# Four products of the unit matrix at the top of each step of attention, up to the ninth batch

## What is computed

```python
x = x + 0.5 * ffn(layernorm(x), gate_w, expert_bias, w1, w2, w3)
x = x + attn(layernorm(x), Wq, Wk, Wv, Wo)
x = x + 0.5 * ffn(layernorm(x), gate_w, expert_bias, w1, w2, w3)

# attn: 16 heads of 8 features, no mask
q, k, v = (x @ W.T, split in heads)
out = softmax(q @ k.T / sqrt(8)) @ v ; return out @ Wo.T
```

## Time and profile before

| | us |
|---|---|
| median of three runs | 1030.36 (1030.28 to 1030.74) |
| the profiled execution | 1034.95 |
| its span, first to last instruction | 1033.1 |
| TensorE products busy | 694.8 |
| VectorE busy | 525.0 |
| ScalarE busy | 356.0 |
| GpSimd busy | 308.2 |
| mean granted clock of TensorE | 0.833 |

### The profile page before, as it was taken

The page is one execution under the profiler, slowest core; times in us unless marked ns, Lnnn a source line. Parts: engine busy times, 40 slices in busy tenths (PEclk is TensorE's granted clock), DMA queues, the critical chain, the costliest instruction groups (busy, mean ns, idle before and its releaser), DMA issues. The chain is left out here.

```text
span 1033.1 us, 14916 instructions
## 1 busy us (share of the span) xinstructions
PE 694.8 (67%) x5124; PEld 501.0 (48%) x5124; DVE 525.0 (51%) x1350; ACT 356.0 (34%) x780; POOL 308.2 (30%) x309
## 2 busy tenths in 40 slices
PE   1335787991589427878989877657687797169900
PEld 1324676981579303434444443323476796158800
DVE  5664277330144327887878889922438632024301
ACT  0001231430134203756777565327232242024300
POOL 4235322437520660001000100340232344651065
PEclk9998787995789655988999897769898899579955
DMA  4133453862466442423333342112165485256432
GB/s 116 31 111 91 112 149 90 221 187 68 127 170 182 110 127 72 143 74 109 109 107 111 93 133 88 38 34 88 38 154 141 118 225 170 49 155 188 139 97 71
DMA packets 104987, 119.74 MB, mean 116 GB/s; under 512 B 11152, under 2 KB 87440, under 8 KB 104912
## 3 DMA queue, kind: packets, MB, share of 16 engines
q1 hardware_dynamic: 87376, 95.95, 32.2%
q0 software_dynamic: 9088, 18.63, 7.7%
q10 hardware_dynamic: 8448, 4.20, 1.4%
HBM read 87.28 MB, written 31.20 MB: 115 GB/s over the span
## 5 line engine op out<-in xcount | busy, mean ns | idle before, releaser
L544 POOL DMA_INDIRECT xe<-normed_rows,idx x156 | 153.2, 982 | 292.1 <-DVE idx L430 147.2
L901 DVE TENSOR_REDUCE mx<-banks 128x2 f32<-128x512 f32 x256 | 164.4, 686 | 41.2 <-remote 15.9
L837 ACT ACTIVATE PT<-banks 128x512 f32<-128x512 f32 x256 | 141.1, 601 | 104.9 <-PE banks L809 92.3
L700 DVE TENSOR_TENSOR hidT<-banks,act 96x256 f32<-96x256 f32 (+1 forms) x92 | 34.9, 379 | 245.5 <-ACT act L671 191.7
L556 POOL DMA_INDIRECT rows<-slots_out,slot x128 | 122.8, 959 | 115.5 <-DMA slots_out<-ye 77.0
L638 PE MATMUL banks<-WR,hidT 128*128 128x128 f32 x936 | 125.6, 283 | 26.0 <-ACT ye L679 23.1
L616 PE MATMUL banks<-xeT,WR 128*128 128x256 f32 (+1 forms) x368 | 97.1, 392 | 52.8 <-issue 52.3
L638 PEld LDWEIGHTS banks<-WR,hidT 128*128 128x128 f32 x936 | 117.3, 199 | 30.2 <-issue 28.2
L796 PE MATMUL banks<-KS,QS 56*128 56x256 bf16 x256 | 75.5, 307 | 69.0 <-DVE mx L901 57.3
L516 POOL TENSOR_TENSOR rough<-var,half_power 128x16 f32<-128x16 f32 x6 | 17.6, 2928 | 309.3 <-DVE var L252 309.3
L616 PEld LDWEIGHTS banks<-xeT,WR 128*128 128x128 f32 x368 | 65.8, 214 | 60.0 <-issue 55.6
(11 more groups left out here) (153 smaller groups left out, 972.1 us busy)
## 6 DMA issues: line engine op xcount, KB each, us to landing
WR<-in_experts SPq DMA_DIRECT2D x92, 544.0 KB
stacks<-split SPq DMA_DIRECT2D x32, 384.0 KB
slots_out<-ye SPq DMA_DIRECT2D x64, 128.0 KB
QS<-stacks SPq DMA_DIRECT2D x64, 112.0 KB
KS<-stacks SPq DMA_DIRECT2D x64, 112.0 KB
normed_rows<-xn ACTq DMA_DIRECT2D x16, 256.0 KB, 2.3
xe<-normed_rows,idx POOLq DMA_INDIRECT x156
rows<-slots_out,slot POOLq DMA_INDIRECT x128
```

Of the source, the lines that this page charges most:

```text
L544: eng.indirect_dma_start(xe[:, i % XR, a, :], None, normed_rows[h], bass.IndirectOffsetOnAxis(ap=idx[h][:, tile:tile + 1], axis=0))\
L837: eng.activation(PT[:, u % 4, 1 - k].rearrange("p t n -> p (t n)"), PS[f % 3], ACT.Exp, scale=scale).then_inc(s_exp2, 1)
L901: eng.tensor_reduce(mx[:, :, e, pair], PS[3 + e][:, :].rearrange("p (q n) -> p q n", q=2), AX.X, ALU.max).then_inc(s_max, 1)
```

## The change

At the top of each step, ahead of its scores, TensorE multiplies the unit matrix with itself four times, while n is below 9. With n from -3 to 8 and eight steps that is 12 x 8 x 4 = 384 products of 128 x 128 x 128 in bf16, each with its own weight load. They write the first 128 columns of bank 7; nobody reads them, they carry no semaphore of their own, and in those rounds nothing else uses the bank. No other instruction is added, taken away or reordered. In the lines behind it the numbers rise by 3 (L796 is L799 in the changed kernel).

```diff
@@ -718,6 +718,9 @@
                 for u in range(PAIRS):
                     if now and u == 0:
                         eng.wait_ge(s_mrow[n % 3], 32 * (n // 3 + 1))
+                    if n < NB + 1:
+                        for _ in range(4):
+                            eng.matmul(PS[7][:, 0:P], identb[:], identb[:], start=True, stop=True)
                     for k in range(2):
                         largest = largest_scores(eng, maxima_of(n, u), k)
                         scores = head_scores(eng, n, u, k) if now else iter(())
```

## The result

The changed kernel took 1039.93 us, the median of 8 runs, against 1031.40 for the kernel before beside it: a ratio of 1.0068, 95% interval 1.0042 to 1.0094. Forecast were 5.8 us less; measured were about 7 us more, outside the range. A second measurement gave 1.0057 (1.0026 to 1.0087), so the sign is not in doubt.

What follows compares the result with a forecast made beforehand. No engine was full; TensorE's clock fell in most attention rounds, and VectorE bound round 2. Sum 5.2 - 0.45 + 0.7 + 0.3 = 5.75 us gained, 1030.36 to 1024.6 us; range 1019.5 to 1031.5.

Steps and rivals of the forecast that it cites:

- The clock: TensorE in rounds 1 and 3 to 8: the added products keep full clock; 5.2 us gained in six rounds; chance 0.70.
- Rival C: Rounds 1 to 8, u = 2 to 4: products don't count for the clock, falls stay; about 5 us lost, 1035.3; chance 0.14.
- D: Clock falls move to half of the rounds instead of going away; 1.8 us gained, 1028.6; chance 0.10.
- The products' own time: Each step's four products on TensorE: 0.06 us each, 0.25 us for four at full clock.
- their place: Products on the path at u = 1 and 7, 0.2 us each, and u = 5, 0.05; elsewhere hidden; 0.45 us a round.
- the row of 24: Products in a row at the start, at half clock: about 2.4 us, delaying the second batch's L739 to some 353.5.
- The rounds 1 to 8: Attention rounds: 5.2 us gained in six rounds, 0.45 lost in round 7, 0.7 gained in round 2.
- The six rounds that had falls: Rounds 1, 3, 4, 5, 6 and 8: from 1.31 above round 7's time to 0.45 above; 5.2 us gained.
- round 7: The round already at full clock throughout, 15.90 us: it loses 0.45 us to the products.
- round 2: Round bound by VectorE: products hidden, clock may still fall once or twice; 0.3 to 1.2 us gained, 0.7 taken.
- The rounds -1 and 0: Rounds partly at half clock: it rises sooner, but products stand before scores; 0.7 us lost to 1.2 gained, 0.3 gained taken.
- The start: Second batch's turn slips, but what follows waits for transfers and doesn't feel it: nothing, up to 0.5 us lost.

Runs made afterwards that it cites:

- early_third: Changed kernel with the four products only in the rounds -3 and -2: 1039.31 us against 1036.47 for the kernel before, ratio 1.0030.
- after: The changed kernel with all 384 products, first measurement: 1039.93 us against 1031.40 for the kernel before, ratio 1.0068.
- after_timed: The changed kernel with all products, timed again: 1038.68 us against 1035.93 for the kernel before.
- late_third: Changed kernel with the four products only in the rounds -1 to 8: 1031.10 us against 1036.47 for the kernel before, ratio 0.9958.
- before: The kernel before, without the products, as in the forecast's trace: median 1031.40 us, profiled execution 1034.95 us.
- hidden_again: Changed kernel with products only at u = 2, 3 and 4 of the rounds -1 to 8: 1027.09 us against 1036.47 for the kernel before, ratio 0.9903.
- two_places: Changed kernel with products only at u = 3 and 4 of the rounds 0 to 8: 1020.96 us against 1028.95 for the kernel before, ratio 0.9912.
- no_burst_again: Changed kernel without the twenty products at u = 3 to 7 of round -3: 50.70 us for the rounds -3 and -2, against 44.3 before.
- burst_only: Changed kernel with only the twenty products at u = 3 to 7 of round -3: 1037.54 us against 1029.66 for the kernel before, ratio 1.0053.
- eight_products: Changed kernel with eight products instead of four at each step: 90.3 us from the first L739 to round 1, 86.22 for rounds 4 to 8.

## Why the prediction was wrong

**The clock** was right. The fall stayed away in all rounds from 1 to 8, at 1.00, and came back where the products were left out (0.90 in four of the rounds 4 to 8 of early_third). Rival C, that these products don't count for the clock, is refuted, and so is D. The Trainium skill ("TensorE: Matmul & The Clock Gate", "Part 4: PE-mode transpose") says that transposes don't count as activity in the same way; plain products of a unit matrix do, by these rows; whether transposes don't, no run here shows. The prediction says that the part with the fall has no such turns; it has (L758 at 502.57 us), and they tell nothing either way.

**The products' own time** was right, their place less so. By their rows four of them take 0.39 us together and one 0.219. The first row is the new line's, with the shortest, median and longest product in ns; the others are TensorE's in round 7 at u = 7 of the changed kernel, in order of time:

```profile
L723 PE MATMUL banks<-identb x384: 217/219/315, 337.2 to 559.9; 128*128 128x128 bf16 x192
```

```profile
543.00 0.44 PE L779 MATMUL banks<-CT,on 128*128 128x128 f32 x2
543.27 0.39 PE L723 MATMUL banks<-identb 128*128 128x128 bf16 x4
543.59 0.28 PE L799 MATMUL banks<-KS,QS 56*128 56x256 bf16 x1
```

The same page ("Back-to-back issue gap") has 81 ns for each; the 57 ns here, (0.39 - 0.22) / 3, decide, and the row of 24, which ran at full clock too and not at half as foreseen, gives 56, (1.50 - 0.22) / 23. A round cost 0.61 instead of 0.45, because two groups meet in the wait at u = 7. Its own group puts the scores 0.59 us behind the start of the turn (543.00 to 543.59), which were 0.37 behind it before (543.72 to 544.09): 0.22 more. The group of u = 6 had pushed the values that the turn follows: they start 1.62 us behind the second L774 now (540.38 to 542.00), 1.45 behind the second L771 before (541.27 to 542.72): 0.17 more. Of these 0.39 us VectorE had 0.05 to spare, and 0.34 passes on where the sum had 0.2.

**The rounds 1 to 8** gained 6.9 us where 5.45 were in the sum (5.2 - 0.45 + 0.7). The six rounds that had falls gained 5.0 instead of 5.2 (0.7 to 0.9 each, and 1.1 in round 3), round 7 lost 0.61 instead of 0.45, and round 2 gained 2.5 instead of 0.7: VectorE did 1.0 us less of side work in it, and idled 0.35 us instead of 1.9. How much there is to gain hangs on the falls that the other kernel happens to have: the six traces without products in these rounds took 139.6 to 143.4 us, so against the least of them 3.1 us are gained. The forecast's trace was the one with most to gain.

**The rounds -1 and 0** together were 0.1 (after) and 0.9 us (after_timed) longer on the late kind, 1.7 on the other; 0.3 gained was in the sum.

**The start** is the step that failed. The prediction put it at "nothing, up to 0.5 us lost" on the ground that what follows the second batch's turn waits for transfers, and that until 388 us "the reductions come at a pace that neither TensorE nor its clock sets". The rounds -3 and -2 cost 10.0 us more in the traces. Without that the traces would have given a gain of some 5.7 us (10.1 - 4.4), about the forecast; that so near a number comes out is in part luck, since round 2 gained 1.8 more than forecast and the rounds 9 to 11 took 1.2 back. late_third, which leaves just these products out, gained 4.4 us by its ratio and 5.4 by the medians. The sentence on the pace was true of TensorE's work, not of its signals, and it was the warning. VectorE's reductions there started 1.5 to 3.5 us behind the scores that TensorE had finished, and the profile had no producer for it:

```profile
367.16 0.69 DVE L901 TENSOR_REDUCE mx<-banks 128x2 f32<-128x512 f32 x1 [2.32 <-remote]
...
375.56 0.69 DVE L901 TENSOR_REDUCE mx<-banks 128x2 f32<-128x512 f32 x1 [4.20 <-remote]
```

I took that stretch as a cover that would be there whatever I did, when it was a state in which a hand-over from TensorE could come late by any time. In the changed kernel two hand-overs to ScalarE, L742 to L849 and L747 to L854, came 18.9 and 14.3 us late, one behind the other, where the same two of the kernel before came on time and behind a transfer; before, it was the reductions that suffered, 1.5 to 3.5 us each. The ten us go with what VectorE had done by then. In the traces of before, late_third, hidden_again and two_places 7 to 11 reductions had started by the end of the last gather; with early products it was none in six traces, one in no_burst_again and three in burst_only. What was not done by then had to be done behind it: from the end of the last gather to round 1 it took 34.5 to 39.2 us in the first four traces and 41.0 to 51.3 in the other eight.

**The range** didn't include this either: no rival had the start as its place, though the waits called remote stood in the trace of the kernel before. Its lower end is also mis-added: the terms named make 12.3 us, which is 1018.1 and not 1019.5. That changes nothing here, as the time lies above the range.

## What to carry to other kernels

Filler products can hold TensorE's clock, and in the rounds 4 to 8 two groups of four in the emptiest part of a round did it as well as eight groups; put them only where the engine waits in any case, since each of them on the path costs its own time in every round. Before you call a stretch a cover, ask what ends each wait in it: one that nothing in the profile explains is no cover, it is a risk, and a change that adds work to it needs a trace, if possible from more than one chip.

## What the runs showed of the hardware

The two kinds of chip differ by 125 us for the same kernel, with the same busy times (VectorE 525.0 and 523.1 us, GpSimd's gather L556 951 and 947 ns at the median). What differs is when TensorE's signals come. The profile's list of waits has lines that name no producer; on the late kind it has them in each of the 12 traces, 191 to 230 us in total, on the other kind in none of the 8. These are two of the twelve in the trace of before, with the total, the number and the longest in us:

```profile
ACT ye L679 <- remote: 47.5, 9, 19.4
...
DVE mx L901 <- remote: 15.9, 5, 4.2
```

By the semaphore events of that trace 56 signals came over 1 us behind the end of the work that they tell of. All 56 are TensorE's, and all came while GpSimd issued gathers or at most 5.3 us behind one. The same holds in the other traces of the late kind, with 49 to 63 of them and 5.5 us at most; on the other kind there is none. Hand-overs from VectorE and ScalarE in the same stretch were taken up within 0.05 us (L905 behind L854, L750 behind L891). In the rounds -3 and -2 of the late kind TensorE's came up to 31.2 us late: in eight_products the second batch's turn ended at 352.87, and

```profile
384.04 0.37 ACT L849 COPY xaT<-banks 128x256 f32<-128x256 f32 x1 [38.62 <-remote]
```

Outside the stretches with gathers both kinds run a full round at full clock in 15.88 to 15.90 us.

Why a few products more make such signals later is open. It goes with their number (82.9, 85.9 and 90.3 us to round 1 with two, four and eight, one trace each but for four), and it needs neither the row of 24 nor the groups around the turn. All that is shown is of products that write bank 7 with weights of their own; whether another kind of work on TensorE would do the same was not tried. Nor was the kernel run without the profile's records, so whether the signals are as late without them is open too.
